# Between the passes of a graph layer: accumulators cleared by ScalarE instead of GpSimd, a leaky step with one relu fewer, an earlier mixing matrix, and a clamped arrival count

## The reference, cut to what matters

```python
def _hconv(x, W, b, src, dst, n):
    xt = x @ W
    D = segment_sum(ones, src);  B = segment_sum(ones, dst)      # counts
    Dinv = where(D > 0, 1 / D, 0);  Binv = where(B > 0, 1 / B, 0)
    m = segment_sum(xt[src], dst) * Binv[:, None]
    out = segment_sum(m[dst], src) * Dinv[:, None]
    return out + b
h = prelu(hconv(xn, W1, b1), a)          # prelu(z) = where(z >= 0, z, a * z)
h = hconv(h, W2, b2) + xn
...
dots = einsum('bhnd,bhne->bhde', k, v)   # per head
out  = einsum('bhnd,bhde->bhne', q, dots) / n, then @ Wout.T + bout
```

## Time and profile before

| what | us |
|---|---|
| median of three runs | 5858.4 |
| the profiled execution, own time | 5866.34 |
| its span, first to last instruction | 5864.6 |
| busy: PE / DVE / ACT / POOL | 4113.0 / 3605.1 / 1255.1 / 3860.7 |
| indirect gathers of the four passes (POOL, line 597), 3324 of them | 3206.0 |
| share of the chain that ended last: PE / DVE / DMA / issue / POOL | 40% / 15% / 14% / 10% / 8% |

### The profile page before, as it was taken

How to read it: one execution, slowest core, us unless ns; L and a number is a source line. 1 busy time by engine, 2 the same in 40 slices (tenths; PEclk the granted TensorE clock), 3 DMA queues, 4 the chain that set the end, 5 groups by cost and what they waited for, 6 DMA issues and landing times.

```text
span 5864.6 us, 68260 instructions
## 1 busy us (share of the span) xinstructions
PE 4113.0 (70%) x16858; PEld 2694.3 (46%) x16859; DVE 3605.1 (61%) x11329; ACT 1255.1 (21%) x3285; POOL 3860.7 (66%) x3972
## 2 busy tenths in 40 slices
PE   4799799999975776777465555555566555557994
PEld 2555466665643444444344334333434434444662
DVE  7788788888876666566755554574555554454324
ACT  0388455555520000000100000000000000222331
POOL 2777777777776777777477777767777777003442
PEclk9899899999998999999787887887787777768997
DMA  3400233333334333333344444444333333411125
GB/s 123 133 2 2 59 100 102 102 100 101 100 104 137 112 112 112 113 112 111 112 139 136 136 140 137 136 143 142 105 105 106 105 105 105 134 53 41 63 64 161
DMA packets 322692, 616.69 MB, mean 105 GB/s; under 512 B 79716, under 2 KB 199096, under 8 KB 321848
## 3 DMA queue, kind: packets, MB, share of 16 engines
q0 software_dynamic: 182400, 464.97, 27.8%
q1 hardware_dynamic: 127932, 133.60, 6.9%
q10 hardware_dynamic: 12028, 14.28, 0.7%
HBM read 525.55 MB, written 87.01 MB: 104 GB/s over the span
## 4 chain that ended last, share of the span: by engine, by line
PE 40%; DVE 15%; DMA 14%; issue 10%; POOL 8%; SPq 1%; ACT 1%; DVEq 1%; ACTq 0%; PEldq 0%; POOLq 0%; PEld 0%
PE PS L1558 19%; POOL rowset L597 8%; PE PS L1482 7%; DVE rowset L1070 7%; DMA rowset<-table,idx 7%; PE PS L1740 3%; PE PS L1764 3%; PE PS L1596 3%; DMA region<-xn_d 2%; DMA skip_d<-region 2%; DVE ohg L1079 2%; PE PS L1634 2%; DMA region<-xt_d 1%; PE PS L1757 1%; DMA rowset<-ye_d 1%
## 5 line engine op out<-in xcount | busy, mean ns | idle before, releaser
L597 POOL DMA_INDIRECT rowset<-table,idx x3324 | 3206.0, 964 | 1088.3 <-issue 706.1
L1558 PE MATMUL PS<-rowset,ohg 128*128 x7040 | 2074.4, 437 | 925.1 <-issue 335.0
L1070 DVE TENSOR_TENSOR rowset<-rowset,PS 128x257 f32 (+1 forms) x3520 | 1478.0, 420 | 1482.0 <-PE PS L1558 1461.5
L1558 PEld LDWEIGHTS PS<-rowset,ohg 128*128 128x128 f32 x7040 | 1436.8, 215 | 1567.7 <-issue 1358.7
L1079 DVE TENSOR_SCALAR ohg<-iota,dl 128x128 f32<-128x128 f16 x2640 | 793.9, 301 | 91.7 <-issue 91.7
L1482 PE MATMUL PS<-region 128*128 128x416 f16 x3328 | 653.3, 339 | 0.0
L605 POOL DMA_INDIRECT scattered_d<-rowset x384 | 372.2, 969 | 132.9 <-issue 121.3
L1482 PEld LDWEIGHTS PS<-region 128*128 128x128 f16 x3328 | 324.5, 98 | 256.9 <-issue 0.9
L692 ACT ACTIVATE region<-region 128x128 f16<-128x128 f16 x832 | 334.1, 402 | 453.9 <-DVE region L994 431.7
L993 DVE TENSOR_SCALAR region<-iota_c,region 128x832 f16<-128x832 f16 x832 | 380.5, 457 | 22.9 <-issue 22.7
L693 ACT ACTIVATE region<-region 128x128 f16<-128x128 f16 x832 | 321.0, 386 | 0.0
(11 more groups left out here) (322 smaller groups left out, 3530.2 us busy)
## 6 DMA issues: line engine op xcount, KB each, us to landing
rowset<-table,idx POOLq DMA_INDIRECT x3324, 2.8
table<-rowset SPq DMA_DIRECT2D x21, 896.0 KB, 5.1
region<-xt_d SPq DMA_DIRECT2D x98, 128.0 KB, 2.2
rowset<-ye_d SPq DMA_DIRECT2D x12, 1024.0 KB, 7.5
xpad_d<-rowset SPq DMA_DIRECT2D x1, 6272.0 KB, 20.7
xn_d<-rowset SPq DMA_DIRECT2D x49, 128.0 KB
xt_d<-rowset SPq DMA_DIRECT2D x49, 128.0 KB
table<-rowset SPq DMA_DIRECT2D x49, 128.0 KB
```

What stands on the lines that cost most here:

```text
L597: gp.indirect_dma_start(rowset[:, at + c % ring, 0:F], None, tables[p], bass.IndirectOffsetOnAxis(idx[p % 2][:, c:c + 1], 0)).then_inc(s_g ...
L1070: TT(a, a, chunk_sum(p, k), ALU.add).then_inc(s_acc[p], 1)
L1558: m = MM(chunk_sum(p, k), ohg[:, k, :], rowset[:, ds(slot_of[k], 1), 0:width(p)].rearrange("p a f -> p (a f)"), start=True, stop=True)
```

## The change

The memset of the first accumulator stays on GpSimd. The other three are taken from it, with GpSimd's waits for the end of the pass before them. ScalarE clears instead, in seven Copy activations of seven blocks (128 x 1799 elements), with a column of zeros as a broadcast input: for pass 1 and pass 3 as soon as the pass before has ended, for pass 2 one piece after each relu of the leaky step. The leaky step uses z + (1 - a) relu(-z), which equals relu(z) - a relu(-z), so relu(z) in place is gone. VectorE clears `mx["dots"]` ahead of the leaky steps, ScalarE copies its blocks before the first relu, and the two PSUM copies of the mixing matrix stand behind the fourth and the sixth piece. TensorE takes the maximum of the arrival count and 1 in a register before each wait. The lower bound that is declared for the loaded counts goes from 1 to 0. The diff shows GpSimd's part first, then ScalarE's, VectorE's and TensorE's.

```diff
-            def memset_acc(p):
-                gp.memset(accs[p % 2][:, :, :], 0.0).then_inc(s_zero, 1)
...
-            memset_acc(0)
+            gp.memset(accs[0][:, :, :], 0.0).then_inc(s_zero, 1)
...
             for p in range(1, 4):
-                pool.wait_ge(s_acc[p - 1], U + PAIR)
                 pool.wait_ge(s_idx, 2)
-                memset_acc(p)
                 pool.wait_ge(s_tab, p * 16 * NR7)
                 gather_pass(p)
...
+            def clear(p, n):
+                return A(accs[p % 2][:, n * R7:(n + 1) * R7, :], z16[:, 0:1].unsqueeze(2).broadcast_to([P, R7, FC]), ACT.Copy)
+            act.wait_ge(s_acc[0], PAIR + U)
+            for n in range(NR7):
+                m = clear(1, n)
+            m.then_inc(s_zero, 1)
...
-            for n in range(NR7):
-                act.wait_ge(s_hz, n + 1)
-                if n >= 2:
-                    act.wait_ge(s_fin, NR7 + n - 1)
-                a = accs[1][:, n * R7:(n + 1) * R7, 0:F]
-                A(negative[n % 2], a, ACT.Relu, scale=-1.0)
-                A(a, a, ACT.Relu).then_inc(s_hr, 1)
             act.wait_ge(s_dz, 1)
             act.wait_ge(s_dots, 1)
...
-            act.wait_ge(s_pp, 1)
-            A(mx["pp"]..., PS[:, 0:2, :]..., ACT.Copy).then_inc(s_ppc, 1)
-            act.wait_ge(s_gm, 1)
-            A(gmat..., PS[:, 3, :], ACT.Copy, scale=1.0 / N).then_inc(s_gmc, 1)
+            for n in range(NR7):
+                act.wait_ge(s_hz, n + 1)
+                if n >= 2:
+                    act.wait_ge(s_fin, NR7 + n - 1)
+                A(negative[n % 2], accs[1][:, n * R7:(n + 1) * R7, 0:F], ACT.Relu, scale=-1.0).then_inc(s_hr, 1)
+                m = clear(2, n)
+                if n == NR7 - 1:
+                    m.then_inc(s_zero, 1)
+                if n == 3:
+                    act.wait_ge(s_pp, 1)
+                    A(mx["pp"]..., PS[:, 0:2, :]..., ACT.Copy).then_inc(s_ppc, 1)
+                if n == 5:
+                    act.wait_ge(s_gm, 1)
+                    A(gmat..., PS[:, 3, :], ACT.Copy, scale=1.0 / N).then_inc(s_gmc, 1)
+            act.wait_ge(s_acc[2], PAIR + U)
+            for n in range(NR7):
+                m = clear(3, n)
+            m.then_inc(s_zero, 1)
...
-            link(TS(nega, a_col[:, 0:1], -1.0, None, ALU.mult))
+            V.memset(mx["dots"], 0.0).then_inc(s_dz, 1)
+            link(TS(not_a, a_col[:, 0:1], -1.0, 1.0, ALU.mult, ALU.add))
...
-                STT(out=a, in0=negative[n % 2], scalar=nega, in1=a, op0=ALU.mult, op1=ALU.add).then_inc(s_fin, 1)
+                STT(out=a, in0=negative[n % 2], scalar=not_a, in1=a, op0=ALU.mult, op1=ALU.add).then_inc(s_fin, 1)
...
             leaky(NR7 - 1)
-            V.memset(mx["dots"], 0.0).then_inc(s_dz, 1)
...
-                    blk_row[p % 2][2:3, i * U + AG - 1:(i + 1) * U:AG], engines=(mybir.EngineType.PE,), min_val=1, max_val=NAG,
+                    blk_row[p % 2][2:3, i * U + AG - 1:(i + 1) * U:AG], engines=(mybir.EngineType.PE,), min_val=0, max_val=NAG,
...
+            at_least = pe.alloc_register("at_least")
...
                         if k % IB == 0:
-                            pe.wait_ge(s_arr[p], arrived[k // AG])
+                            pe.reg_alu(at_least, pe.to_reg(arrived[k // AG]), 1, ALU.max)
+                            pe.wait_ge(s_arr[p], at_least)
```

More of the change, by code:

```diff
@@ L239, in gps_layer @@
         nch, endc, first, mean_c, rstd_c, var_c, tmp_c = (small[:, k, :] for k in range(7))
-        nega = small[:, 7, 0:1]
+        not_a = small[:, 7, 0:1]
         row_number = small[:, 7, 1:2]
@@ L745, in _ @@
             m.then_inc(s_dcp, 1)
-            act.wait_ge(s_pp, 1)
-            A(mx["pp"].rearrange("p a b -> p (a b)"), PS[:, 0:2, :].rearrange("p a b -> p (a b)"), ACT.Copy).then_inc(s_ppc, 1)
-            act.wait_ge(s_gm, 1)
-            A(gmat[:, :, :].rearrange("p a b -> p (a b)"), PS[:, 3, :], ACT.Copy, scale=1.0 / N).then_inc(s_gmc, 1)
+            for n in range(NR7):
[8 more added lines that the diff above has]
+                    act.wait_ge(s_pp, 1)
+                    A(mx["pp"].rearrange("p a b -> p (a b)"), PS[:, 0:2, :].rearrange("p a b -> p (a b)"), ACT.Copy).then_inc(s_ppc, 1)
+                if n == 5:
+                    act.wait_ge(s_gm, 1)
+                    A(gmat[:, :, :].rearrange("p a b -> p (a b)"), PS[:, 3, :], ACT.Copy, scale=1.0 / N).then_inc(s_gmc, 1)
+            act.wait_ge(s_acc[2], PAIR + U)
+            for n in range(NR7):
+                m = clear(3, n)
+            m.then_inc(s_zero, 1)
             def fold_gamma(i, k):
```

## The result

Over twenty runs of each, the changed kernel takes 5851.88 us (median; 5845.62 to 5863.24), the kernel before 5866.34 us (5855.3 to 5872.72). The ratio is 0.9976 with a 95% interval of 0.9970 to 0.9982: 14 us faster (11 to 18), where 21.2 us were forecast. In absolute terms the forecast of 5837.2 us is 14.7 us too low, and its range (5830 to 5850) misses by 2.

What follows compares the result with a forecast made beforehand. The prediction took GpSimd's gathers to pace all four passes, with the work between passes added whole. Savings of 10.4, 11.0 and 0 us, less 0.2, made 21.2: from 5858.4 to 5837.2 us, range 5830 to 5850.

Steps and rivals of the forecast that it cites:

- the places: Stretches between passes, last add to first gather: savings of 10.4, 11.0 and 0 us forecast.
- The clamp: TensorE's register maximum before each of 880 waits: a cost of 0.2 us in all, at the ends of the passes.
- four passes run at GpSimd's pace: GpSimd's gathers pace all four passes, waiting only 0.3 us in gaps; what comes between passes is added whole.
- The base: Median of the kernel before, taken as 5858.4 us, 7.9 us below the profiled execution.
- The lock: Between passes, GpSimd's memset holds VectorE's tensor_scalar on shared ports: 10.59 and 10.66 us, against 0.2 when free.
- The first place: Between passes 0 and 1: 10.4 us saved once the tensor_scalar is no longer held.
- third place: Between passes 2 and 3: saving 0, since VectorE isn't held and GpSimd waits for the table.
- The second place: Between passes 1 and 2: 11.0 us saved, from 10.5 + 1.9 (one relu) - 0.5 (matrix clear) - 0.9 (table stores).
- The stores' 0.9: Table stores between passes 1 and 2: 0.7 us lost to closer last pieces, 0.2 to three loads behind them.
- The rival with TensorE as the pace of pass 0: Register steps before TensorE's 220 waits in pass 0 add 42 us, net +21: 5879 us; chance 0.04.
- Rival 2: One place gains, the other gives it back through loads in flight or slow clears: some 11 us, 5847; chance 0.1.

Runs made afterwards that it cites:

- memset_later: Kernel before plus TensorE's register maximum, with GpSimd's memsets for passes 1 and 2 held until VectorE's reciprocal is done: 5853.44 us, ratio 0.9963.
- pool_touch: Changed kernel with a one-element GpSimd memset between its waits for the indices and for the table: 7287.12 us, one run, where the kernel before takes 7308.
- the third sitting: Session of four runs, among them the kernel before plus TensorE's register maximum (ratio 1.0010); the kernel before takes 7308 us there.
- clamp_only: Kernel before plus only one register maximum ahead of each of TensorE's 880 waits for arrivals: 5877.46 us, ratio 1.0010.
- clamp_x16: Changed kernel with sixteen register maxima in the source ahead of each TensorE wait instead of one: 5859.29 us, ratio 0.9988.
- clamp_early: Changed kernel with a turn's four register maxima taken together right behind the loads of the counts: 5850.12 us, ratio 0.9966.
- prefetch_b: Changed kernel with two buffers for the rows of k and v in pass 1, loaded a turn sooner, on another chip: 5841.70 us, ratio 0.9948.
- mix_late: Changed kernel with the mixing matrix made behind the leaky steps, as in the kernel before: 5856.14 us, ratio 0.9966.
- combined: Kernel before plus GpSimd memsets behind VectorE's reciprocal, one relu, register maxima behind the count loads; mixing matrix late: 5843.38 us, ratio 0.9958.

## Why the prediction was wrong, point by point

The mechanism of the gain was right, its size was not. Against the forecast 21.2 us the profiles show 14.2: the places gave 19.8 where 21.4 were put (1.6 short), and the passes grew by 5.6 where the clamp's 0.2 were put (5.4 short). The step that failed is the overlap of the passes, "four passes run at GpSimd's pace", by which nothing that TensorE or VectorE lose in a pass could reach the time. The runs showed in its place that pass 1 ends at TensorE's and VectorE's pace, 14.4 us behind the last gather and 8.5 with earlier loads; which cost made up the 5.6 stays open. The base, three runs, was 7.9 us too low on top of that; with it alone right, the forecast would have been 5845.1, inside its range but still 6.7 below the measured time.

**The lock** was right, term by term. Read from before: 10.59 and 10.66; after: 0.20 and 0.20, the value chosen. memset_later shows it with the memset kept on GpSimd. The sentence of the Trainium skill ("SBUF — State Buffer", "Who interferes with whom") that a tensor_scalar can meet GpSimd on the shared ports while a two-input instruction is bothered by its reads only was borne out by both as far as a memset, which only writes, can show it; no run here has GpSimd read beside them. Its other sentence, that the first to issue gets the pair, stays unproven here: at the first place the memset's row began first, by 0.04 us, as the sentence has it, but at the second the tensor_scalar's began 0.03 us ahead and was held all the same.

**The first place**: forecast -10.4, measured -9.9. The missing 0.5 us is what pool_touch names: with the memset gone, GpSimd has nothing between its waits, and its first gather starts 0.73 us and not 0.26 behind the last landing. This is also why the **third place** grew by 0.48 us, where 0 was forecast. The change has a cost there and no gain.

**The second place**: forecast -11.0, measured -10.3. The two waits for the second relu are gone (no gap at the first leaky step, 4.07 us for the last two), ScalarE's copies fit. The stores' 0.9 is a sum of 0.7 for their closeness and 0.2 for the three loads behind them. The first came as forecast: with the matrix late the last store lands 0.7 us later than before (4.8 against 4.03). The second was mis-sized: with the matrix early, and the loads right behind the store, it lands 0.6 later still. With the 0.5 us of GpSimd's wait that is 0.9 too much, and 0.2 more gain than forecast ahead of the last store leaves the missing 0.7.

**The clamp** is a term that seems mis-sized: 0.2 us forecast. "No row shows one" was a misreading; the kernel before has such instructions in a later stage:

```profile
L1738 PEldq ALU_OP  x108: 32/32/32, 5331.5 to 5778.2; - x108
```

Three comparisons of the kernel before with the clamp alone give 1.0010, 1.0010 and 1.0017, the first two with 1 just outside, the second of them in the third sitting. 6 us fits them, and 19.8 - 6 = 13.8 fits the change's 14. Against it stand memset_later, which has the clamp and no shortfall, and the profile of clamp_only, whose passes are no longer than before. Its duration explains 1 to 2 us of the 6 (clamp_x16), and placing it elsewhere didn't clearly help (clamp_early). So what made the passes 5.6 us longer stays open, between the clamp and the luck of one execution; the kernel before has one profile, which leaves its passes with one sample. The rival with TensorE as the pace of pass 0 is out: the 0.185 us more of clamp_x16 would have added 220 * 0.185 = 41 us to pass 0 if nothing hid them, and pass 0, first gather to last add, reads 1109.9 us against 1101.7 and 1103.9 in the changed kernel.

**What bounds the kernel** is the step that failed in kind. "Four passes run at GpSimd's pace" was read from waits of 0.3 us, and GpSimd indeed never waits long. That doesn't say that the pass ends with GpSimd. In pass 1 the rows for k and v are loaded once per 16 arrivals, while TensorE needs them once per 16 pairs, and 831 chunks make 880 pairs; so TensorE is held back more with each turn. The last load is issued 963 us after the first gather, and 90.3 us from there to the last add (before: load at 2745.76, last add ended 2836.08) are TensorE's and VectorE's own: TensorE waits for arrivals 3.5 of them. With the load a turn sooner the tail drops by 6 to 10 us (prefetch_b). So in this stretch a small delay of TensorE or VectorE should count in full, which no run tried by itself: it is 90.3 us before and 90.8 to 94.6 in eleven profiles with the clamp, a spread that also holds luck. This could hold the 2.7 us of pass 1, not the 2.5 us of pass 2. The rows to have read were the chain in the last 100 us of pass 1 and the 13.49 us of GpSimd's idle time ahead of the second memset in the earlier trace rows, against 6.24 in the earlier trace rows.

**The base.** The forecast took the terms against the profiled execution, 5845.1 us in its frame, and moved the sum to the median of three runs, 5858.4, since the profiled one (5866.34) stood above all three. Twenty runs put the median at 5866.34. The three were the lowest three of the twenty, so they weren't like the others. A range that follows three runs has to hold such a shift too: 8 us here.

**Rival 2**, a part of the gain given back, comes nearest to what happened; its 5847 us came from a gain of 11, where 14 was measured, and a base 8 too low, and its mechanisms (loads in flight, slow clears) weren't the ones.

## What to carry to other kernels

Read what ends each stage, not only whether the busiest engine waits: an engine that never waits can finish 14 us ahead of the stage's end, as GpSimd did in pass 1, and then small costs on the others may be paid in full. If a short VectorE instruction is exactly as long as a GpSimd one beside it, ordering the two by one semaphore is enough; moving the work to a third engine isn't needed and here was slower by 1 us at the places (88.2 in mix_late, 87.1 in combined). And before extra instructions are used as a yardstick, count their rows: the sixteen maxima of the source were three instructions in the trace. Where a buffer is refilled once per unit of one count and used once per unit of another (chunks and pairs), let the refill run ahead.

## What the runs showed that was not expected

- In one sitting every kernel, the one before too, ran 25% slower (7308 us), and the stretches between the passes there had the length that they have elsewhere to 0.1 us.
- The gathers of pass 0 alone differ by 19 us between two executions of one kernel on two chips (1088.1 and 1107.5), those of pass 3 by 2.8 (1038.3 and 1041.1).
